# Who multiplies slot 9's states by C: GpSimd or VectorE, in a pipelined Mamba and mixture-of-experts block

## The reference

```python
def step(h, inp):                                   # h: 256 channels x 16 states for each sequence
    dt_t, B_t, C_t, x_t = inp
    dA = jnp.exp(dt_t[..., None] * A[None])
    h = dA * h + (dt_t * x_t)[..., None] * B_t[:, None, :]
    y = jnp.einsum('bdn,bn->bd', h, C_t)            # product with C, then a sum over the 16 states
    return (h, y)
...
x = x + 0.5 * ffn(layernorm(x))
x = x + mamba(layernorm(x))
x = x + 0.5 * ffn(layernorm(x))
```

## Time and profile before

| what | value |
|---|---|
| median of 3 runs | 1376.2 us (1373.83 to 1384.54) |
| the profiled execution's own time | 1375.99 us |
| its span, first to last instruction | 1374.2 us |
| mean granted clock of TensorE | 0.895 of full speed |
| from one chunk's slot 9 to the next one's, middle of the program | 75.62 and 74.29 us in turn |
| instructions of the product: VectorE L774 | 352, 692 ns each |
| instructions of the product: GpSimd L956 | 80, 2361 ns each |

### The profile page before, as it was taken

The page is one execution under the profiler, slowest core; times in us unless marked ns, Lnnn a source line. Parts: engine busy times, 40 slices in busy tenths (PEclk is TensorE's granted clock), DMA queues, the critical chain, the costliest instruction groups (busy, mean ns, idle before and its releaser), DMA issues.

```text
span 1374.2 us, 16300 instructions
## 1 busy us (share of the span) xinstructions
PE 1159.3 (84%) x5188; PEld 586.0 (43%) x5188; DVE 1061.5 (77%) x1713; ACT 876.8 (64%) x1171; POOL 1066.3 (78%) x900
## 2 busy tenths in 40 slices
PE   2778776878999989898989999898989896966787
PEld 1344332434454545354445445354445443423355
DVE  2021888988888898988888898889898889989910
ACT  0343847577767777686777676776867776664532
POOL 1024898998888998988988899989898889998600
PEclk9998887999898999899998999899989998968687
DMA  3004133323233240423332323304132323232000
GB/s 91 1 0 180 47 130 94 131 92 119 99 124 108 66 165 23 147 83 131 102 128 87 133 100 99 134 28 158 64 130 95 130 93 132 94 138 85 1 8 16
DMA packets 60405, 130.02 MB, mean 95 GB/s; under 512 B 7744, under 2 KB 26864, under 8 KB 52128
## 3 DMA queue, kind: packets, MB, share of 16 engines
q1 hardware_dynamic: 60320, 128.98, 27.2%
HBM read 106.94 MB, written 22.02 MB: 94 GB/s over the span
## 4 chain that ended last, share of the span: by engine, by line
PE 59%; DVE 19%; ACT 8%; POOL 6%; issue 6%; SPq 1%; ACTq 0%; DVEq 0%; DMA 0%; POOLq 0%
PE PY L483 17%; PE PH L468 14%; PE G L457 9%; PE Y L495 7%; DVE dA L770 7%; PE PH L467 4%; DVE hb L768 4%; PE G L523 3%; DVE hb L774 3%; PE G L449 2%; POOL hb L948 2%; DVE stat L749 1%; POOL xr L931 1%; PE PY L481 1%; ACT L666 1%
## 5 line engine op out<-in xcount | busy, mean ns | idle before, releaser
L948 POOL TENSOR_TENSOR hb<-dtx_rep,bs 128x1024 f32<-128x1024 f32 x256 | 598.9, 2361 | 0.0
L770 DVE TENSOR_TENSOR_SCAN dA<-dA,hb 128x512 f32<-128x512 f32 x352 | 429.1, 1219 | 20.7 <-ACT dA L644 13.4
L644 ACT ACTIVATE dA<-dt_rep,A 128x512 f32<-128x512 f32 x512 | 343.7, 690 | 114.0 <-DVE hb L774 94.7
L607 ACT COPY hs<-PH 128x512 f32<-128x512 f32 x256 | 149.3, 583 | 297.5 <-PE PH L468 297.3
L468 PE MATMUL PH<-xnT,W 128*128 128x512 f32 x512 | 315.3, 700 | 0.0
L483 PE MATMUL PY<-W,hs 128*128 128x128 f32 x2048 | 301.8, 292 | 0.0
L483 PEld LDWEIGHTS PY<-W,hs 128*128 128x128 f32 x2048 | 264.3, 197 | 82.9 <-issue 71.8
L774 DVE TENSOR_TENSOR hb<-dA,cs 128x512 f32<-128x512 f32 x352 | 243.5, 692 | 24.8 <-DVE dA L770 0.5
L956 POOL TENSOR_TENSOR hb<-hb,cs 128x1024 f32<-128x1024 f32 x80 | 188.9, 2361 | 76.8 <-DVE hb L768 76.7
L768 DVE TENSOR_TENSOR_SCAN hb<-dA,hb 128x512 f32<-128x512 f32 x160 | 186.4, 1206 | 8.9 <-ACT dA L644 6.7
L495 PE MATMUL Y<-hb,Sel 128*32 128x512 f32 x1024 | 163.3, 715 | 29.3 <-POOL hb L956 21.0
(11 more groups left out here) (85 smaller groups left out, 1180.9 us busy)
## 6 DMA issues: line engine op xcount, KB each, us to landing
dtx_rep<-dtx_rows SPq DMA_DIRECT2D x32, 1024.0 KB, 6.4
dt_rep<-dt_rows SPq DMA_DIRECT2D x32, 1024.0 KB, 7.7
bs<-bc_rows SPq DMA_DIRECT2D x64, 256.0 KB, 3.6
cs<-bc_rows SPq DMA_DIRECT2D x64, 256.0 KB, 4.2
dtx_rows<-dtx SPq DMA_DIRECT2D x32, 256.0 KB, 2.5
dt_rows<-dt SPq DMA_DIRECT2D x32, 256.0 KB, 2.6
X<-in_x SPq DMA_DIRECT2D x16, 256.0 KB, 3.0
out<-X SPq DMA_DIRECT2D x16, 256.0 KB, 2.4
```

The costliest lines, as they stand in the source:

```text
L607: nc.scalar.copy(hs[:, w, e, :], PH[:, :]).then_inc(ph_free, 1)
L644: nc.scalar.activation(dA[u % NA][:, :], dt_rep[:, h, g, :], ACT.Exp, scale=A[:, h, g, q:q + 1]).then_inc(decay, 1)
L770: nc.vector.tensor_tensor_scan(a, a, x_in_hb, 0.0, ALU.mult, ALU.add).then_inc(scan, 1)
L948: nc.gpsimd.tensor_tensor(hb[:, s % HR], dtx_rep[:, h, 2 * m:2 * m + 2, :], bs[:, q, None, :].broadcast_to([P, 2, CH]), ALU.mult).then_inc ...
```

## The change

GpSimd no longer makes the product with C of slot 9's pair; VectorE makes it, one unit at a time, behind each of the two scans.

```diff
-POOL_C = (1, 2, 5, 9, 14)
+POOL_C = (1, 2, 5, 14)
 NP = len(POOL_C)
 NV = UN - 2 * NP
```

## The result

The changed kernel takes 1383.74 us (median of 6 runs, 1381.87 to 1385.53) against 1377.89 (6 runs, 1373.83 to 1384.54): 1.0048 of the time before, interval 1.0029 to 1.0067. The two medians lie 5.9 us apart. The profiled execution's span is 1381.9 us, against 1374.2, 7.7 us more; each of these two spans is that of a single execution.

What follows compares the result with a forecast made beforehand. It took the chain of work, 59% on TensorE, and not a full engine to set the time; 0.9 + 2.1 + 4.6 = 7.6 us on the profiled 1375.99 us gave 1383.6 us, range 1374 to 1393.

Steps and rivals of the forecast that it cites:

- What is taken from GpSimd is worth nothing: GpSimd at slot 9: removing 2.35 us a chunk, 37.6 us in all, only lengthens its idle time before the root; worth 0.
- The rival of 3.4 us in chunk 13: Near the program's end, TensorE's 3.40 us wait for slot 9's product comes back, giving 1380.2 us; chance 5%.
- The price on VectorE, 1.54 us a chunk: VectorE at slot 9: a pair with products takes 3.79 us, one only scanned 2.25; the difference is 1.54 us.
- The cover of 1.26 us in chunks 2 to 12: VectorE's wait for TensorE's products into PY hides most of the added work; 0.08 us a chunk remains, 0.9 us in all.
- the rival of 24.6 us: VectorE becomes the bound: the cover moves off and all 16 chunks pay 1.54 us, giving 1400.6 us; chance 9%.
- Chunks 0 and 1, 2.1 us: First two chunks at slot 9: thinner idle cover of 0.40 and 0.43 us, so 1.06 and 1.03 us are exposed.
- Chunks 13 to 15, 4.6 us: Last three chunks: the chain runs through VectorE's slot 9 without a wait, so each pays the whole 1.54 us.
- Contention: Less GpSimd work could make VectorE's instructions faster; the prediction took 0, with VectorE's product at 0.69 us either way.
- The clock as a rival of its own: Middle chunks' split between 75.62 and 74.29 us changes: 1390.3 us if slower (chance 8%), 1375.6 if faster (12%).
- the prediction's own signs: Right if middle chunks stay 75.6 and 74.3 us and the last three each grow 1.5; another split means the clock.
- The Trainium skill's rule: Busiest engine is the bottleneck: VectorE ends 17.3 us above where GpSimd stood, giving 1393.3 us; weighed within the 9% rival.

Runs made afterwards that it cites:

- e3: The changed kernel plus a GpSimd instruction the size of the product it gave up, into an unread tile; 1383.52 us, 1.0038 of the kernel before.
- e10: Against the kernel before, VectorE makes slot 9's product in chunk 13 only; 1379.33 us, 0.9973 of the kernel before.
- e1: Against the kernel before, VectorE makes slot 9's product in chunks 2 to 12 only; 1380.65 us, 1.0023 of the kernel before.
- e4: The changed kernel plus one more unread VectorE product for each unit of slot 9 in chunks 2 to 12; 1385.06 us, 1.0057 of the kernel before.
- e6: The changed kernel plus two more unread VectorE products for each unit of slot 9 in chunks 2 to 12; 1403.23 us, 1.0130 of the kernel before.
- e11: Against the kernel before, VectorE makes slot 9's product in chunks 14 and 15 only; 1383.26 us, 1.0002 of the kernel before.
- e12: Against the kernel before, VectorE makes slot 9's product and GpSimd makes slot 10's instead; 1422.54 us, 1.0297 of the kernel before.

## Why the prediction was right, point by point

The time (1383.6 said, 1383.74 measured), the sign and the size (7.6 us said, 5.9 between the medians, 7.7 between the traces) lie where they were forecast. Its steps did not all carry their part, and the exact agreement is luck.

- *What is taken from GpSimd is worth nothing.* Shown twice: its idle time ahead of the root went from 25.6 to 51.9 us (4.7 each, as said), and a dummy instruction in its place changed nothing that shows (e3). The rival of 3.4 us in chunk 13 fell too: TensorE waits there for VectorE instead.
- *The price on VectorE, 1.54 us a chunk.* Right: from slot 9's first scan to y it is 3.80 us in chunk 3 (402.37 to 406.17), as put together from slot 10's rows, and in chunk 13, where nothing covers it, the add comes 1.56 us later (e10). Its busy time rose by 20.4 us instead of the 22 said.
- *The cover of 1.26 us in chunks 2 to 12.* Right in the trace (0.11 us left over, 0.08 said), and the rival of 24.6 us is refuted by e1. That the cover is used up is shown by e4: the next 1.19 us come out behind the add in full.
- *Chunks 0 and 1, 2.1 us.* Right on VectorE's way: in e3, e4 and e6, which have the change's own edit there, the two stretches from dtx to dtx took 1.0 and 1.1 us more than before (74.35 and 74.89 in e3, against 73.33 and 73.81). In the changed kernel's own trace the clock moved there too and left 0.7 us of it.
- *Chunks 13 to 15, 4.6 us.* This is the term that was mis-sized: 6.8 us in the trace, 5.3 in chunk 13 and 1.5 in the other two together. 1.54 us of the 5.3 are VectorE's; the rest, 3.8 us, goes with TensorE's stay at 1.2 GHz. By e10 and e11 that is no fixed cost of the edit.
- *Contention.* None seen: VectorE's product took 692 ns before and after.
- *The clock as a rival of its own.* I gave it 20% and took it for a matter of which middle chunks are the slow ones. It is no rival but is at work in every trace: it took back 0.8 us of the middle, added to the end, and made 4.3 us between two executions of the same code (e11). By the prediction's own signs this case came true: the middle chunks no longer take 75.6 and 74.3 us in turn, and the last three aren't each 1.5 us longer. What should have stood in its place is a range around each term. That the clock also makes the two groups of the kernel before isn't shown, since no run of the second group has a trace.
- *The Trainium skill's rule.* To take the engine with the highest occupancy for the bottleneck (Perfetto Trace Analysis, Identifying the Most-Contended Engine) gave 1393.3 by VectorE's new load. The trace bears it out neither for the relief of GpSimd (e3) nor for VectorE: 20.4 us more of busy time cost 5.9 us, and 12 more in e4 cost 1.5. With another 13 us (e6) it is 18 us over the kernel before.

What stays open: by what the clock places its slow stretches. The runs show only that small shifts move them, and that TensorE stood idle for 2 us or more close by. That alone doesn't decide: in the changed kernel TensorE is idle for 2.8 us ahead of 413.86 in chunk 3 and ahead of 488.26 in chunk 4, and only the first is beside a slow stretch. So the sign of the change and VectorE's part are shown; how much of the 5.9 us is the edit's and how much the clock's is not.

## What to carry to other kernels

Price a moved instruction by the idle time right behind it on the engine that gets it and right ahead of the next thing on the engine that gives it; busy shares say nothing about either. Of a product that is handed to another engine, ask first where it comes in that engine's list and who reads it when: the same 2.35 us were free at slot 9 and cost 6 us a chunk at slot 11. And where TensorE is nearly on the path, compare chunks at the same granted clock (here 73.09 us at 1.00) before comparing times, since the clock can hide a real cost or pass for one; a trace of a kernel whose edit leaves that place alone (here e11) tells how far it moves by itself.

## What the runs showed of the hardware

- The same chunk of work took 73.09, 74.40 and 75.96 us at a granted clock of 1.00, 0.95 and 0.91. A stretch at 1.2 GHz costs by its place: 6.8 us of it, 7 us behind the add, cost nothing (e4), 3.4 us of it 45 us behind the add cost 1.3, and 10 us around xr cost 1.5.
- The same code with the same arrival of xr took 67.54 us in one trace and 71.84 in another (e11), with TensorE at 1.2 GHz for 13.7 and for 20.5 us of it.
- Making TensorE wait 1 us longer for xr cost up to 6 us a chunk (e12, 80.5 us against 74.3), with TensorE at 1.2 GHz for 14 us afterwards; where it was 7 us, the chunk took 76.5.
- An identical program moved between 1374.9 and 1386.0 us from run to run and had medians of 1376.8, 1383.4 and 1384.1 us on three chips. The Trainium skill, TensorE: Matmul & The Clock Gate, The HAM clock gate, says that the number of slow matmuls at the start of one and the same kernel varies from run to run (6, 11 or 14). The traces here show slow stretches that move in the middle and at the end too; that they make the spread of the times isn't shown.
